# Attention's first four batches in two pairs: batches 0 and 1 loaded, projected and evacuated ahead of 2 and 3, whose low parts come by a matmul with -1 and a ScalarE copy

## What is computed

```python
def xattn(X, ctx, ...):          # X = layernorm(x); 32 heads of 8, 8 groups of keys/values
    q = X @ Wq.T + bq            # 256 wide: (group, head in group, 8)
    k = ctx @ Wk.T + bk          # 64 wide
    v = ctx @ Wv.T + bv          # 64 wide
    scores = einsum('bgrqd,bgkd->bgrqk', q, k) / sqrt(8)
    scores = where(mask_qk | mask_pad, -inf, scores)
    out = einsum('bgrqk,bgkd->bgrqd', softmax(scores), v)
    return out @ Wo.T + bo
x = x + tanh(g_xattn) * xattn(layernorm(x), ctx, ...)
x = x + tanh(g_ffn) * experts(layernorm(x), ...)   # 16 experts of 96, best 2 of each token
```

## Time and profile before

| | |
|---|---|
| median of 3 runs | 242.26 us (242.17 to 242.55) |
| the profiled execution | 242.28 us, its span 240.5 us |
| granted TensorE clock, mean | 0.997 |
| PE busy | 220.8 us, 92% of the span |
| DVE, ACT, POOL busy | 71%, 40%, 39% |
| first scores (first `scores_q`) | 19.29 us |
| slot 0 (first `scores_k`) | 29.62 us |

### The profile page before, as it was taken

One profiled execution on the slowest core, in us unless ns is written; L12 is line 12 of the kernel. 1 busy time (PEld: TensorE's weight loads), 2 busy tenths in 40 slices (PEclk: granted clock), 3 DMA queues, 4 the chain that ended last, 5 costly groups with the idle time before them and its releaser, 6 DMA issues.

```text
span 240.5 us, 3821 instructions
## 1 busy us (share of the span) xinstructions
PE 220.8 (92%) x1279; PEld 159.1 (66%) x1279; DVE 170.2 (71%) x355; ACT 96.7 (40%) x190; POOL 94.8 (39%) x127
## 2 busy tenths in 40 slices
PE   0688798989999999999999899999999899999993
PEld 0675563565555555546466778879898798888892
DVE  2578978658777878785832678659984888774665
ACT  2456358756676767665776210110101111011000
POOL 6239325400608393937301021307996363320000
PEclk9999999999999999999999999999999999999998
DMA  6372320008761202020203100042546222123105
GB/s 186 102 235 57 78 55 22 4 0 180 170 149 29 60 8 67 1 65 9 59 8 131 46 0 0 5 140 64 147 114 189 94 87 81 52 46 88 44 0 174
DMA packets 26274, 18.33 MB, mean 76 GB/s; under 512 B 15600, under 2 KB 22320, under 8 KB 26256
## 3 DMA queue, kind: packets, MB, share of 16 engines
q1 hardware_dynamic: 25952, 17.87, 27.4%
q10 hardware_dynamic: 304, 0.22, 0.4%
HBM read 14.15 MB, written 1.11 MB: 63 GB/s over the span
## 4 chain that ended last, share of the span: by engine, by line
PE 70%; DVE 9%; POOL 7%; DMA 5%; ACT 3%; issue 3%; SPq 1%; ACTq 0%; DVEq 0%; POOLq 0%
PE bank L1019 64%; DMA wkv_n<-in_L_xattn_Wv 2%; DVE mneg L879 2%; POOL cT L551 2%; POOL w_d L555 2%; DMA w_t<-comb_d 2%; PE bank L1079 2%; POOL cT L550 2%; DVE pT L947 1%; POOL w_d L554 1%; ACT q L616 1%; DVE x_sb L1012 1%; DMA q<-q 1%; DVE q L953 1%; PE bank L1059 1%
## 5 line engine op out<-in xcount | busy, mean ns | idle before, releaser
L1019 PE MATMUL bank<-xT,cT 128*128 128x512 f32 x288 | 70.7, 393 | 1.0 <-DVE pT L939 0.7
L1019 PEld LDWEIGHTS bank<-xT,cT 128*128 128x128 f32 x288 | 52.6, 188 | 12.4 <-issue 1.2
L879 DVE TENSOR_REDUCE mneg<-bank 128x4 f32<-128x512 f32 x64 | 43.0, 684 | 11.6 <-PE bank L1019 10.6
L683 ACT ACTIVATE pT<-bank 128x512 f32<-128x512 f32 x24 | 14.4, 599 | 78.5 <-PE bank L1019 78.5
L696 ACT ACTIVATE pT<-bank 128x512 f32<-128x512 f32 x64 | 37.9, 599 | 18.8 <-PE bank L1019 17.8
L1019 PE MATMUL bank<-w_d,q 128*128 128x256 f32 x288 | 38.6, 284 | 1.7 <-issue 0.9
L1019 PEld LDWEIGHTS bank<-w_d,q 128*128 128x128 f32 x288 | 37.0, 190 | 4.5 <-issue 3.1
L1019 PE MATMUL bank<-q,kz 112*128 112x512 f32 x64 | 37.5, 586 | 0.0
L1019 PE MATMUL bank<-kz,q 96*128 96x512 f32 x64 | 26.5, 420 | 2.4 <-DVE mneg L879 1.8
L939 DVE TENSOR_TENSOR pT<-pT,bank 128x512 f32<-128x512 f32 x24 | 16.4, 684 | 17.1 <-PE bank L1019 15.2
L1019 PE MATMUL bank<-ident_b,cmask 128*128 128x512 bf16 x64 | 24.5, 383 | 1.2 <-ACT pT L696 0.6
(11 more groups left out here) (127 smaller groups left out, 278.3 us busy)
## 6 DMA issues: line engine op xcount, KB each, us to landing
w_t<-comb_d SPq DMA_DIRECT2D x16, 192.0 KB, 2.8
w_t<-comb_d SPq DMA_DIRECT2D x16, 128.0 KB, 2.9
padf<-in_L_ffn_down_w SPq DMA_DIRECT2D x12, 128.0 KB, 2.3
c_sb<-in_ctx SPq DMA_DIRECT2D x2, 512.0 KB, 6.5
q<-cT SPq DMA_DIRECT2D x8, 128.0 KB, 2.4
w_t<-comb_d SPq DMA_DIRECT2D x16, 64.0 KB, 2.7
out<-x_sb SPq DMA_DIRECT2D x4, 256.0 KB, 2.4
c_sb<-in_L_ffn_gate_w SPq DMA_DIRECT2D x8, 96.0 KB, 2.1
```

Source lines behind the costliest of these rows:

```text
L683: nc.scalar.activation(act_g[:, n % 2], bank[0][:], ACT.Silu).then_inc(a_ok, 1)
L879: nc.vector.tensor_reduce(mneg[:, r, 4 * hf:4 * hf + 4], bank[SQ_BANK[n % 3]][:].rearrange("p (g k) -> p g k", g=4), X, ALU.max, negate=Tr ...
L1019: return nc.tensor.matmul(dst, a, b, start=start, stop=stop, skip_group_check=True)
```

## The change

- `PHASE_A` has jobs of two batches. The near jobs `cn`, `xn`, `kvn`, `qn` serve batches 0 and 1; one transposing job covers both feature blocks, and projections are 256 columns wide. The far jobs `cf`, `xf`, `kv`, `q` serve 2 and 3.
- SP loads x of batches 0 and 1, then their context, Wq, the query-key mask, x of 2 and 3, the bias rows, the padding mask, the context of 2 and 3, the gates and bo. Before, it was x (0, 1), x (2, 3), context (0 to 3), Wq, the bias rows, the gates, bo, the padding mask and the query-key mask.
- DVE takes the statistics of tiles 0 and 1 first; those of 2 and 3 come behind xn's low part, their normalisation behind the near keys.
- A far job's low part no longer is DVE's. PE adds to the bank, which still holds the sum, the high part times -1 (`subtract_high`, with `ident_w`, a negative identity that POOL fills), and ACT copies the rest out (`far_low`). The high part of the far queries has a tile of its own, `qf_hi`.
- The far jobs stand between the score pairs on PE; the small matmuls after a pair go, but for those after pair 1, and there are 20 and 12 instead of 24 and 18 in two other places.
- `RAMP` changes: pairs 16 to 20 come one to three slots later.

The core of the diff:

```diff
-RAMP = (8, 9, 11, 13, 15, 17, 19)
+RAMP = (8, 9, 11, 13, 15, 16, 16, 18, 20)
...
-        PHASE_A = [("wkv",), ("c", 0, 0), ("c", 0, 1), ("wq",), ("x", 0, 0), ("x", 0, 1), ("bias",), ("kv", 0),
-                   ("q", 0, 0), ("q", 0, 1), ("MT", 0)]
+        PHASE_A = [("wkv",), ("cn",), ("xn",), ("wq",), ("bias",), ("kvn",), ("qn", 0), ("qn", 1),
+                   ("cf",), ("xf",), ("kv", 0), ("q", 0, 0), ("q", 0, 1), ("MT", 0)]
+        FAR_JOBS = [("cf",), ("xf",), ("kv", 0), ("q", 0, 0), ("q", 0, 1)]
...
-        A_BANK = (2, 3, 4, 5, 6, 7, 2, 4, 3, 6, 7, 7)
+        A_BANK = (2, 3, 4, 5, 6, 7, 2, 3, 4, 6, 4, 6, 7, 4)
...
             sp.dma_start(x_sb[:, 0:2, :], x[0:2].rearrange("b p d -> p b d")).then_inc(d_x0, 16)
+            sp.dma_start(c_sb[:, 0:2, :], ctx_in[0:2].rearrange("b p d -> p b d")).then_inc(d_c0, 16)
+            sp.dma_start(wq_n[:], Wq.rearrange("(o p) d -> p o d", p=P)).then_inc(d_wq, 16)
+            sp.dma_start(mqk_u[:], m_qk).then_inc(d_mask, 16)
             sp.dma_start(x_sb[:, 2:TPH, :], x[2:TPH].rearrange("b p d -> p b d")).then_inc(d_x, 16)
-            sp.dma_start(c_sb[:, 0:TPH, :], ctx_in[0:TPH].rearrange("b p d -> p b d")).then_inc(d_ctx, 16)
-            sp.dma_start(wq_n[:], Wq.rearrange("(o p) d -> p o d", p=P)).then_inc(d_wq, 16)
...
+            sp.dma_start(pad_u[:], m_pad.rearrange("(a b) k -> a (b k)", a=1).to_broadcast([P, NB * L])).then_inc(d_mask, 16)
+            sp.dma_start(c_sb[:, 2:TPH, :], ctx_in[2:TPH].rearrange("b p d -> p b d")).then_inc(d_ctx, 16)
...
-            sp.dma_start(pad_u[:], m_pad.rearrange("(a b) k -> a (b k)", a=1).to_broadcast([P, NB * L])).then_inc(d_mask, 16)
-            sp.dma_start(mqk_u[:], m_qk).then_inc(d_mask, 16)
...
-            inverse_deviation(0, 0, TPH)
+            inverse_deviation(0, 0, 2)
             pool.wait_ge(pool_init, 2)
             for sub in range(2):
                 pool.memset(vz[:, :, sub::2, 16 * sub + HD:16 * sub + HD + 1], 1.0)
             pool.memset(mt[:].bitcast(F32), 0.0)
+            pool.tensor_scalar(ident_w[:, 0:QR], ident[:, 0:QR], 0.0, None, ALU.mult).then_inc(pool_init, 1)
+            pool.tensor_scalar(ident_w[:, QR:QR + P], ident, -1.0, None, ALU.mult).then_inc(pool_init, 1)
             pool.tensor_copy(ident_b[:], ident).then_inc(pool_init, 1)
+            inverse_deviation(1, 2, 2)
...
+            def far_low(j):
+
+                sc.wait_ge(far_sub, FAR_JOBS.index(j) + 1)
+                ps, k = jbank(j), j[0]
+                if k in ("cf", "xf"):
+                    ins = nc.scalar.copy((cT if k == "cf" else xT)[1][:, :, FAR], ps[:].rearrange("p (c n) -> p c n", c=DC))
+                elif k == "kv":
+                    nc.scalar.activation(k4[2 * QR:3 * QR, 0, FAR], ps[0:QR, FAR], ACT.Identity, bias=bias[0:QR, 2 * R:2 * R + 1])
+                    ins = nc.scalar.activation(k4[2 * QR:3 * QR, 1, FAR], ps[QR:2 * QR, FAR], ACT.Identity,
+                                               bias=bias[QR:2 * QR, 2 * R + 1:2 * R + 2])
+                else:
+                    ins = nc.scalar.activation(qc_lo[:, j[2], FAR], ps[:, FAR], ACT.Identity,
+                                               bias=bias[:, 2 * R + 3 + j[2]:2 * R + 4 + j[2]])
+                ins.then_inc(far_lo, 1)
+
...
+            for j in PHASE_A[0:4]:
+                high(j)
+            sc.wait_ge(d_gate, 32)
+            nc.scalar.activation(tg[:], gate[:], ACT.Tanh).then_inc(tg_ok, 1)
+            sc.wait_ge(*emptied(("bias",)))
+            sc.wait_ge(pool_init, 1)
+            sc.wait_ge(job_done, jn["kvn",] + 1)
+            keys_near_high()
+            queries_near_high(0)
+            take_values(("kvn",), NEAR, NEAR)
+            queries_near_high(1)
+            high(("cf",))
+            high(("xf",))
+            far_low(("cf",))
+            far_low(("xf",))
+            high(("kv", 0))
+            take_values(("kv", 0), FAR, FAR)
+            high(("q", 0, 0))
+            far_low(("kv", 0))
+            high(("q", 0, 1))
+            far_low(("q", 0, 0))
             high(("MT", 0))
+            far_low(("q", 0, 1))
 
...
-            for t in range(TPH):
-                if t == 2:
-                    ve.wait_ge(d_x, 16)
-                own(nc.vector.bn_stats(stats[:, t], x_sb[:, t]))
-            settle()
-            for t in range(TPH):
-                ins = nc.vector.bn_aggr(mv[:, t], stats[:, t])
-            ins.then_inc(var_ok, 1)
+            statistics(0, 2)
             take(("wkv",))
-            normalise(0, 0, TPH)
-            take(("c", 0, 0))
-            take(("c", 0, 1))
+            normalise(0, 0, 2)
+            take(("cn",))
+            take(("xn",))
...
-            for c in range(DC):
-                ve.wait_ge(far_hi, 2 + c + 1)
-                queries_low(0, c, FAR)
-            keys_low(FAR, far_hi, 0, k_ok)
...
+            def subtract_high(j):
+
+                ps, k = jbank(j), j[0]
+                pe.wait_ge(job_hi, hn[j] + (2 if k == "kv" else 1))
+                if k in ("cf", "xf"):
+                    for c in range(DC):
+                        ins = mm(ps[:, c * 2 * L:(c + 1) * 2 * L], ident_w[:, QR:QR + P], (cT if k == "cf" else xT)[0][:, c, FAR], False, True)
+                elif k == "kv":
+                    for hf in range(2):
+                        ins = mm(ps[0:2 * QR, FAR], ident_w[0:QR, QR * (1 - hf):QR * (3 - hf)], k4[0:QR, hf, FAR], False, True)
+                else:
+                    ins = mm(ps[:, FAR], ident_w[:, QR:QR + P], qf_hi[:, j[2]], False, True)
+                ins.then_inc(far_sub, 1)
+
...
+            pe.wait_ge(pool_init, 5)
+            pe.wait_ge(*emptied(("wq",)))
+            keep_busy(20)
             pe.wait_ge(mask_ok, 1)
-            pe.wait_ge(pool_init, 3)
-            pe.wait_ge(*emptied(("bias",)))
-            keep_busy(24)
-            for n in range(G):
-                scores_q(n)
-                keep_busy(3)
-            keep_busy(18)
+            scores_q(0)
+            job(("cf",))
+            scores_q(1)
+            keep_busy(3)
+            scores_q(2)
+            job(("xf",))
+            scores_q(3)
+            subtract_high(("cf",))
+            scores_q(4)
+            subtract_high(("xf",))
+            job(("kv", 0))
+            scores_q(5)
+            job(("q", 0, 0))
+            scores_q(6)
+            subtract_high(("kv", 0))
+            job(("q", 0, 1))
+            scores_q(7)
+            subtract_high(("q", 0, 0))
+            pe.wait_ge(max_ok, 6)
+            keep_busy(12)
             job(("MT", 0))
+            subtract_high(("q", 0, 1))
             keep_busy(18)
             for s in range(SLOTS):
                 if s < CH:
```

More of the change, by code:

```diff
@@ L106, in build @@
         ident_b = sb("ident_b", [P, P], BF16)
+        ident_w = sb("ident_w", [P, QR + P], F32R)
         x_sb = sb("x_sb", [P, NB, D])
@@ L300, in build @@
         for j in JOBS:
-            if j[0] in ("wkv", "wq", "wo", "c", "x", "AT", "YT") or j[0] in ("kv", "q") and j[1]:
+            if j[0] in ("wkv", "wq", "wo", "cn", "xn", "cf", "xf", "c", "x", "AT", "YT", "kv", "q"):
                 hn[j] = count
                 count += {"kv": 2}.get(j[0], 1)
-        ln = {j: n for n, j in enumerate(j for j in JOBS if j[0] not in ("MT", "q", "kv"))}
+        ln = {j: n for n, j in enumerate(j for j in JOBS if j[0] not in ("MT", "q", "kv", "kvn", "qn", "cf", "xf"))}
         def emptied(j):
@@ L1109, in job @@
                 ins.then_inc(job_done, 1)
[L1111 removed]
+            for j in PHASE_A[:8]:
                 job(j)
```

170 lines of the change are left out of this document (94 added, 76 removed).

## The result

| | before | after |
|---|---|---|
| median (range) | 242.25 us (242.11 to 242.55, 6 runs) | 244.76 us (243.74 to 245.94, 6 runs) |
| the profiled execution | 242.28, span 240.5 | 244.24, span 242.4 |
| first scores | 19.29 | 20.18 |
| last row maximum ends | 27.17 | 29.43 |
| slot 0 | 29.62 | 31.98 |

The change makes the kernel slower: ratio 1.0104, 95% interval 1.0074 to 1.0135. The prediction was 243.9 in a range of 241.3 to 245.2, with 0.57 on slower. The profiled execution is 1.96 us longer, where the forecast had 1.66. But the runs of after spread over 2.2 us, those of before over 0.4, and the profiled one lies in the lower half. It falls into the forecast's own band (243.0 to 244.7); the median lies 0.06 above that band and nearest to rival C's 244.9.

What follows compares the result with a forecast made beforehand. TensorE was taken to bound the kernel from slot 0 (29.62 us), so earlier delays add on; VectorE bounded the maxima before it. First scores 0.3, score stretch 0.9 and RAMP 0.46 gave 242.28 + 1.66 = 243.9, range 241.3 to 245.2.

Steps and rivals of the forecast that it cites:

- rival C: Projections before the first scores: TensorE also at the lower clock level after pauses, kvn 0.6 us more; 245.4 or 244.9; chance 0.19.
- Step 1: Start of the kernel: value weights Wv land at 7.0 instead of 7.66 us, a gain of 0.66.
- Step 2: Relay from Wv's landing to the first key evacuation: starts at 14.7 instead of 14.96 us, 0.25 saved; ends 14.3 and 15.4.
- Step 3: Key evacuation to first scores: q copy behind SP's loads, scores at 19.6 instead of 19.29, +0.3 us; range 18.6 to 20.2.
- Step 4: First scores to last row maximum: TensorE replaces VectorE as the bound, +0.9 us over 7.88; low end 0.
- Step 5: Changes said to be worth 0, such as VectorE losing far low parts; last maximum to slot 0 stays 2.45 us.
- Step 6: New RAMP in attention slots 5 to 9: late score pairs delay slot 8, +0.46 us, between 0 and 0.9.
- The sum: Whole kernel: 0.3 + 0.9 + 0.46 = 1.66 us added to 242.28, giving 243.9.
- A: Up to the last score pair: PE's extra work stays hidden, under 6.5 us; 241.6 or 241.2; chance 0.24.
- B: Whole kernel: gain and cost cancel, first scores -0.5, score stretch +0.5, RAMP 0.2; 242.5 us; chance 0.17.

## Why the prediction was right, and where not

- **Step 1** (Wv at 7.0, ends 6.56 and 7.66): the early end held, 6.51. The rate of the row was right, its reason only in part. With the order of before and the context in two DMAs Wv lands at 6.96 or 6.28, so by these two runs 0.7 to all of the 1.15 comes from the context's second half being a DMA of its own. I had not weighed that.
- **Step 2** (first key evacuation 14.7): 15.18, within the ends, released by PE as said. With V = 6.51 its relay would give 14.2. Of the 1.0 that is missing, 0.54 are kvn's matmuls, 1.59 in the chain instead of 1.05: the slower rate of rival C holds here, and the run with the small matmuls shows for the q jobs that it hangs on the pause. Another 0.19 is the bias transpose (0.32 with its issue, where I had 0.13), 0.1 is issue behind kvn, and 0.15 is what the relay up to the bias rows took more: xn's four transposes 1.13 where I had 0.9, the rows behind them a little less. The 0.25 that this step counted as saved was not worth anything in the kernel before: there the first scores hung on the q evacuation at 15.95, released by PE, and the run with the early bias copy moved the key evacuation to 14.78 and the first scores not forward at all.
- **Step 3** (first scores 19.6, released by the copy): the size of the copy's term was right, 19.68 and 19.76 where only the normalisation was moved. The step failed in what it left out. I priced the second pair's normalisation nowhere on the path to the first scores, though the diff puts it between the near keys and the near queries on VectorE. By the row of four it would take 0.69 and be hidden under the copy; it takes 1.57, since it meets GpSimd's kz, and so the first scores came at 20.18 by VectorE. rw_n landed at 19.24 in after (issued 12.94, 6.3 to landing), where I had 19.3, but for another reason than I gave: SP issues it 1.58 later than before, since it waits for the far context (1.3) before it goes on. The copy was not held by it, 2.17 where only the normalisation was moved. In the one run where it was held it landed 0.15 behind the last load, not 0.9, so by that the late end of 20.2 was too late.
- **Step 4** (+0.9, 0 to 1.3): the mechanism was right, PE takes VectorE's place. The size was 1.37, just above the end. PE was busy without a gap; up to the start of the last pair the count gave 7.3 to 7.8, and the trace has 7.89 (20.18 to 28.07). The count's high end was the value to take, not its low half.
- **Step 5** (0): the last maximum to slot 0 takes 2.55 instead of 2.45. Right within 0.1 in this profile, but not in every run: the maxima are ready 2.26 later than before and GpSimd's kz of batch 2 starts only 0.70 later (28.98 before, 29.68 now), so that it now stands beside `mt`, and where they meet it costs 0.9. I had looked at ScalarE's work beside this stretch and not at GpSimd's.
- **Step 6** (+0.46, 0 to 0.9; the pairs go one or two slots later, none three): 0.30 by the run with the old RAMP, and from slot 0 to the q job of slot 9 19.47 instead of 19.27, where I had 19.7. The term was too large by 0.16 to 0.26.
- **The sum**: 0.89 + 1.37 + 0.10 + 0.24 (by slot 9) = 2.60, less 0.3 in attention and 0.3 behind it, is 1.96 against 1.66. Steps 3 and 4 were too small by 0.59 and 0.47, step 6 too large, and 0.6 came back that no step spoke of. That the number landed near is partly luck. The median lies 0.5 above the profiled execution, a part of the spread that no trace holds.
- **The rivals**: A fell at the point it named, PE's work up to the last pair took 7.9 and not under 6.5. B fell at its first term: the first scores came 0.89 later and not 0.5 earlier. C's slower rate was there for kvn and the near q jobs, at 0.54 for kvn, and Wv's earlier landing paid for it. Its 244.9 is near the median, but by other sums: its first scores at 19.9 were to hang on the clock and the copy, and hung on the normalisation.

## What to carry to other kernels

When an instruction changes its place, price it by what the other engines run beside it there, not by its row elsewhere; and look on every path for work that the diff slips between two old steps. An engine that is given the work of another needs room for it at that place: here PE's row alone came to 9.25 us where VectorE had needed 7.88. Moving loads earlier was worth nothing here below the time at which the last load of the queue lands, with a later copy in that queue.

## What was not expected of the hardware

- GpSimd's work slows VectorE's in some pairs only. Two normalisations of 128x256 floats take 0.73 to 0.85 alone or beside a uint8 conversion, 1.57 beside kz's two-input float work; a 128x32 cast 0.18 alone, 0.33 and 1.06 beside it, a 128x32 subtraction 0.19 alone, 0.97 beside it. VectorE's low parts, which read PSUM, take 0.48 to 0.49 each in either company. Which operand decides was not tried. The Trainium skill ("GPSIMD Engine Reference", Specifications) says that GpSimd shares its SBUF interfaces with VectorE and contends with VectorE's instructions that are in a 2-port performance mode or have two SBUF inputs. The slowed subtraction, with two SBUF inputs, and the unslowed low parts, with one, agree with that. Whether the normalisation and the cast, with one such input each, run in such a mode, no trace shows; that the normalisation is unharmed beside the uint8 conversion is not foreseen by it.
- Small matmuls meant to keep the clock moved a pause to a worse place, and the lower level came with it, in one trace: 0.53 granted for 3.6 us, 1.2 us behind a pause of 2.58 us.
- A copy issued into a queue of loads landed 0.15 us behind the last load, 3.22 after its issue, where 2.0 to 2.2 is its own time. The far keys' copy, 64 KB as well, took 2.0 to 3.9 from issue to landing over the traces.
